# A graph network on one core: the last stage's affine map moves from VectorE to POOL

## What is computed

```python
def _L1_gnn_ref(x, edge_index, ...):
    ...
    h_new = (1.0 - z) * n + z * x
    mean = jnp.mean(h_new, axis=0)
    var = jnp.var(h_new, axis=0)
    return gamma * (h_new - mean) * jax.lax.rsqrt(var + BN_EPS) + beta
...
x = _layernorm(x + _L1_gnn_ref(x, edge_index, ...), axis=-1)
```

## Time and profile before

| | us |
|---|---|
| median of 3 runs | 1928.1 (1924.65 to 1928.97) |
| the profiled execution, its own time | 1930.21 |
| its span, first to last instruction | 1928.5 |
| VectorE busy in the whole span | 1369.0 (71%) |
| ScalarE busy | 1231.8 (64%) |
| POOL busy | 945.6 (49%) |
| last stage, from the first map to the end | 1726.1 to 1928.5 |
| last stage, groups whose state is loaded | maps from 1726.1 to 1814.1 |
| last stage, groups whose state is kept | maps from 1816.0 to 1914.2 |

### The profile page before, as it was taken

One profiled execution on the slowest core, in us unless ns is written; L12 is line 12 of the kernel. 1 busy time (PEld: TensorE's weight loads), 2 busy tenths in 40 slices (PEclk: granted clock), 3 DMA queues, 4 the chain that ended last, 5 costly groups with the idle time before them and its releaser, 6 DMA issues.

```text
span 1928.5 us, 36544 instructions
## 1 busy us (share of the span) xinstructions
PE 1583.2 (82%) x8258; PEld 1103.0 (57%) x8258; DVE 1369.0 (71%) x4573; ACT 1231.8 (64%) x3127; POOL 945.6 (49%) x911
## 2 busy tenths in 40 slices
PE   5400599999999957999998986999999999976664
PEld 2200387788778845777776764555555555545543
DVE  7916366676666645666666663688888888878897
ACT  0385366666666624666666665677777777757788
POOL 5000566666666636666666662666666666600000
PEclk8855799999999987999999998999999999987898
DMA  8496466653444434777766665687775444439987
GB/s 260 165 340 260 151 191 189 191 175 132 137 137 137 137 120 152 256 251 256 250 201 194 198 200 173 189 227 231 230 210 142 127 126 133 124 111 354 347 282 245
DMA packets 218927, 382.40 MB, mean 198 GB/s; under 512 B 38959, under 2 KB 41228, under 8 KB 218832
## 3 DMA queue, kind: packets, MB, share of 16 engines
q1 hardware_dynamic: 190272, 342.01, 52.4%
q0 software_dynamic: 28560, 39.34, 10.1%
HBM read 222.75 MB, written 177.81 MB: 208 GB/s over the span
## 4 chain that ended last, share of the span: by engine, by line
PE 70%; DVE 11%; issue 7%; DMA 6%; ACT 3%; POOL 1%; SPq 1%; DVEq 1%; another core or an unknown queue 1%; POOLq 0%; ACTq 0%
PE bank L1332 10%; PE bank L1315 9%; PE bank L1307 9%; PE bank L1299 5%; PE bank L1382 5%; PE bank L1368 4%; PE bank L1370 4%; PE bank L1375 4%; PE bank L1374 4%; PE bank L1372 4%; PE bank L1351 3%; DVE gath L1207 3%; PE bank L1354 3%; DVE onehot L1084 2%; PE bank L1294 2%
## 5 line engine op out<-in xcount | busy, mean ns | idle before, releaser
L668 POOL DMA_INDIRECT gath<-XP,ROWI x294 | 298.0, 1014 | 335.0 <-issue 229.7
L668 POOL DMA_INDIRECT gath<-MT,ROWI x294 | 325.7, 1108 | 205.7 <-PE bank L1382 106.6
L668 POOL DMA_INDIRECT gath<-G,ROWI x294 | 294.8, 1003 | 193.7 <-PE bank L1332 96.5
L1332 PE MATMUL bank<-gath,onehot 128*128 128x128 f32 x1176 | 164.2, 292 | 71.6 <-issue 30.8
L1315 PEld LDWEIGHTS bank<-w_sb,page 128*128 128x128 f32 x1568 | 191.0, 192 | 49.3 <-issue 49.3
L740 ACT ACTIVATE page<-bank,b_sb 128x512 f32<-128x512 f32 x196 | 124.1, 684 | 112.3 <-PE bank L1307 90.3
L1315 PE MATMUL bank<-w_sb,page 128*128 128x128 f32 x1568 | 192.0, 275 | 1.7 <-issue 1.7
L1332 PEld LDWEIGHTS bank<-gath,onehot 128*128 128x128 f32 x1176 | 146.0, 200 | 79.2 <-issue 65.0
L1307 PE MATMUL bank<-page,w_sb 128*128 128x512 f32 x392 | 185.7, 596 | 1.6 <-issue 1.6
L1402 PE MATMUL bank<-ident,page 128*128 128x128 f32 x784 | 125.3, 308 | 73.2 <-DMA page<-YT 66.2
L1051 DVE TENSOR_TENSOR page<-bank,DINV 128x512 f32<-128x512 f32 x98 | 67.8, 692 | 155.3 <-PE bank L1315 142.0
(11 more groups left out here) (213 smaller groups left out, 3562.4 us busy)
## 6 DMA issues: line engine op xcount, KB each, us to landing
page<-YT SPq DMA_DIRECT2D x196, 256.0 KB, 4.1
MT<-page SPq DMA_DIRECT2D x98, 260.0 KB
XP<-page SPq DMA_DIRECT2D x98, 256.0 KB, 2.1
G<-page SPq DMA_DIRECT2D x98, 256.0 KB
OWN<-page SPq DMA_DIRECT2D x98, 256.0 KB
page<-OWN SPq DMA_DIRECT2D x98, 256.0 KB
YT<-page SPq DMA_DIRECT2D x98, 256.0 KB
page<-AD SPq DMA_DIRECT2D x98, 256.0 KB
```

The source lines that it names most:

```text
L668: nc.gpsimd.indirect_dma_start(gath[k][:, w, 0:width], None, rows, bass.IndirectOffsetOnAxis(ap=ROWI[:, at:at + 1], axis=0), bounds_check= ...
L1332: last = nc.tensor.matmul(bank[k][:, j * D:(j + 1) * D], onehot[k][:, first:first + P], gath[g.slot(4)][:, w, 0:D], start=(i == 0), stop=( ...
```

## The change

The map leaves VectorE's step function. POOL, behind its last gathers, waits for the scale and the offset (`bn_ok` reaches 2; it reached 1 long before, at line 965), and then maps the 98 groups one after the other, written out without a loop. It waits for the same things as VectorE did: the load of HT in the first 44 groups, and the use of the page four groups back. The last instruction of the small chain now signals `bn_ok` and VectorE no longer waits for its end.

```diff
@@ -694,6 +694,18 @@
             pool.wait_ge(n_agg, NG)
             gathers(2, mt_rows, SUMM, DM, c_agg)
 
+            pool.wait_ge(bn_ok, 2)
+
+            for index in range(NG):
+                g = Group(index // 8, index % 8, unroll=8)
+                k = g.slot(4)
+                if not g.kept:
+                    wait(pool, h_in[k], g.dma(4) + ROUND)
+                wait(pool, o_tr, g.freed(4))
+                nc.gpsimd.tensor_scalar(o_t[k], kept(g) if g.kept else o_h[k], bn[:, 5:6], bn[:, 6:7],
+                                    ALU.mult, ALU.add).then_inc(o_q, 1)
...
@@ -1188,17 +1200,10 @@
...
-            link(nc.vector.tensor_tensor(bn[:, 6:7], gb_sb[:, 1:2], bn[:, 7:8], ALU.subtract))
+            nc.vector.tensor_tensor(bn[:, 6:7], gb_sb[:, 1:2], bn[:, 7:8], ALU.subtract).then_inc(bn_ok, 1)
             wait_all_dmas(dve, h_st, 2, FREE)
 
             def final(group_of):
-                if g := group_of(0):
-                    k = g.slot(4)
-                    if not g.kept:
-                        wait(dve, h_in[k], g.dma(4) + ROUND)
-                    wait(dve, o_tr, g.freed(4))
-                    nc.vector.tensor_scalar(o_t[k], kept(g) if g.kept else o_h[k], bn[:, 5:6], bn[:, 6:7],
-                                            ALU.mult, ALU.add).then_inc(o_q, 1)
                 if g := group_of(2):
```

## The result

The changed kernel takes 1905.93 us in the median of four runs (1902.41 to 1908.61), the kernel before 1926.38 beside it (1922.74 to 1928.97): a ratio of 0.9898, 95% interval 0.9884 to 0.9913, so 17 to 22 us faster, some 20 in the middle. The forecast was 1916, with 1909 to 1928 as its range: the direction was right, the size was not.

The account below looks back on a forecast made before the run. The prediction took transfers to bound the last stage's first half and VectorE its second. Its terms, -12.2 (second half) + 0 (first half) + 0.5 (start) = -11.7 us, took the median from 1928.1 to 1916, range 1909 to 1928.

Parts of the forecast that it names:

- Part 1: Second half, state in SBUF: VectorE loses its maps, 1.03 us a pair, its own period going from 3.72 to 2.69.
- Part 2: Second half: the next limit sets 3.25 us a pair of groups, between 3.10 and 3.40, saving 12.2 us.
- floor of 3.10: Second half: transfers of 1.049 MB a pair at 338 GB/s take 3.10 us, the largest of three floors.
- (c): Loop through YT's four pages, load to TensorE's use: 2.7 us a pair at today's landing, 3.2 at the fuller half's.
- Part 3: POOL's new map instruction: 0.8 us a group, beside a period of 1.6, so zero cost.
- cases of 0.55 and 2.9 us: Other lengths for POOL's map: 0.55 us by the memset's slope, 2.9 by the iota of 784 columns.
- Part 4: First half, 44 groups loaded from memory, and the stage's start: 0 (from -3 to +5) and 0.5 us lost.
- rival E: First half gains 4 per cent of 90 us, as HT's landing no longer blocks VectorE's queue: 1912; chance 0.10.
- The start: Before POOL's first map: an added hand-over and first instruction of its kind, 0.5 us lost, from 0 to 6.
- Rival B: VectorE's short two-input instructions and POOL hold each other up at SBUF: about 1926, chance 0.10; as loss 1943, 0.07.
- C: POOL's map is longer than a group's period, deciding from 1.86 us: 1941 at 2.1 us, 2024 at 2.9; chance 0.05.
- D: Second half: transfers stop the gain earlier, at DMA share 0.92 and 3.47 us a pair: 1923; chance 0.16.

Follow-up runs that it names:

- e1_kept: Kernel before, with POOL mapping only the 54 groups whose state is kept in SBUF and VectorE still mapping the 44 loaded ones: ratio to before 0.9948.
- e2_first: Kernel before, with POOL mapping only the 44 loaded groups and VectorE the 54 kept ones: ratio to before 0.9957, 8.3 us faster.
- e7_deep: Changed kernel with eight pages each for HT and YT instead of four: ratio to before 0.9893.
- e3_late: Kernel before, with VectorE's map moved from the start to the end of its step, without POOL: ratio to before 0.9958, 8.1 us faster.
- e12_phase: Changed kernel, with POOL starting each kept-half map only when VectorE has ended its short instructions: ratio to before 0.9892.
- e4_beside: Kernel before, with POOL also mapping pages of kept state into spare pages, result unused: ratio to before 1.0092, 17.7 us slower.
- e5_twice: Changed kernel with a second, unused POOL map ahead of each real one, 1.54 us for both: ratio to before 0.9989.
- e9_again: Changed kernel measured once more, nothing altered: ratio to before 0.9897.

## Why the prediction was wrong, step by step

- **What bounds the kept half, and Part 1.** Right: VectorE's load did. Taking the map off VectorE's queue there gives 10.0 us (e1_kept), or 11.4 as the difference between the changed kernel and e2_first.
- **Part 2, the next limit.** Near: 3.25 us a pair chosen, 3.04 to 3.28 measured in seven executions; 12.2 us forecast, 10.0 to 11.4 measured in the medians. The floor of 3.10 from the transfers at 338 GB/s was too high: the first profile ran at 3.04, which is ScalarE's 3.01 with next to nothing added, and moved 341 GB/s over its middle (1820 to 1870), while the loaded half shows that the DMA engines can carry some 400. The loop over four pages, (c), costs nothing that can be told (e7_deep).
- **Part 3, POOL's map.** 0.77 us against 0.8, and at that length it costs nothing that shows. The cases of 0.55 and 2.9 us didn't arise. The Trainium skill's 769 ns for 512 elements (GPSIMD Engine Reference, 3.1) is what the trace shows.
- **Part 4, the loaded half and the start.** This is the step that failed. It forecast 0 and +0.5 us and the half with its start gave -8.3 (e2_first). The sentence that failed is "the transfers are full, so little of it can be had". It had named the mechanism, VectorE's statistics queued behind a map that waits for HT, and even its row, 11.2 us of waits, and then capped it at 1 us by the DMA share of 0.99. The share rose to only 1.03 while the rate rose from 355 to 385 GB/s, with a steady part near 400: a share of 0.99 over the half doesn't mean that no more bytes fit. The same trace had slices of 390 and more, which I quoted in rival E and gave a chance of 0.10. E was the case that came true, with 8 per cent more rate in place of 4; the other terms came out near, so this one is what put the time outside the range.
- **The start.** The first map on POOL began 0.11 us after VectorE's last step of bn (1723.24 to 1723.35) and took no longer than the others (two in 1.52 us). The 6 us that the Trainium skill (GPSIMD Engine Reference, 2.1) gives for the first call of a freshly loaded kernel don't show. The first pair of groups is reached sooner, 8.8 and 10.1 us after the first map against 11.5, in e3_late 10.4 too: the same queue order.
- **Rival B, holds at SBUF.** The mechanism is real and its price in the changed kernel is nothing that can be told (e12_phase). It costs 17.7 us where VectorE has no idle time and itself maps (e4_beside).
- **Rivals C and D.** Neither came. C put the point where POOL's length decides at 1.86 us a map. At 1.54 the gain is already nearly spent (e5_twice), more likely by the holds of B than by POOL's pace.

With the measured loaded half in the place of the forecast one, the sum is -12.2 - 8.3 = -20.5, against 19.6 to 20.5 us saved. That it fits so closely is in part luck, since the kept half by itself measured 10.0.

## To carry to other kernels

An in-order engine that waits for a transfer holds back everything behind it, also work whose inputs have long been there. Before moving an instruction to another engine, put it behind the work that is ready: here that alone gave 8 of 20 us, without the other engine. A mean DMA share near 1 is no proof that the transfers bind. Look at the rate in short slices: here it swung between 277 and 405 GB/s where the transfers didn't bind, and stood near 400 where they nearly did. Then follow the chain of waits, and see whether it passes through an engine between a landing and the next issue.

## What the runs showed of the hardware

- POOL's tensor_scalar with two operations and per-partition operands, 128x512 f32 in SBUF, takes 0.77 us; VectorE's 0.55, of which 0.46 to 0.52 show from start to start.
- A VectorE instruction with two SBUF inputs that starts 0.16 to 0.6 us after a map of POOL from SBUF ends 0.01 to 0.02 us after that map (24 of 24 in after and e9_again); most that start earlier in it aren't held (37 of 43). VectorE's map is held too, though it has one tensor input (e4_beside), and a map of POOL that starts behind VectorE's takes up to 1.08 us in place of 0.77. VectorE's statistics from PSUM are not touched (in after 285 ns beside POOL's maps; 284 in before).
- VectorE's map, once POOL's has ended, ends 0.28 us later (41 cases in e4_beside, spread 0.01), half of the 0.55 us that it shows when it runs alone.
- Reads and writes mixed 2 to 1 reach 385 to 390 GB/s over the loaded half, at a DMA share of 1.03 to 1.04, and 400 to 406 in most of its 5 us stretches once it is under way (after, e3_late), where the share reads 1.05 to 1.06.
